# The first layer of the experts as three products of rounded parts, in one transformer block on one core

## What is computed

```python
# 16 experts, cap = 256 rows each, d = 256, H = 1024, all float32
buf = jnp.zeros((n_exp, cap, d), x.dtype).at[idx, safe_pos].add(jnp.where(keep[:, None], xf, 0.0))
h = jax.nn.relu(jnp.einsum('ecd,edh->ech', buf, W1) + b1[:, None, :])
y = jnp.einsum('ech,ehd->ecd', h, W2) + b2[:, None, :]
out = y[idx, safe_pos] * gate[:, None]
```

## Time and profile before

| | |
|---|---|
| median of 3 runs | 1383.31 us (1381.31 to 1388.11) |
| the profiled execution | 1389.05 us, of which the span from first to last instruction 1387.2 us |
| TensorE busy | 1235.2 us (89%) |
| VectorE, ScalarE, GpSimd busy | 824.6, 573.5, 326.3 us |
| mean granted TensorE clock | 0.942 |
| the chain that ended last, by engine | PE 67%, issue 11%, ACT 6%, DMA 5%, DVE 5% |

### The profile page before, as it was taken

The page is one execution under the profiler, slowest core; times in us unless marked ns, Lnnn a source line. Parts: engine busy times, 40 slices in busy tenths (PEclk is TensorE's granted clock), DMA queues, the critical chain, the costliest instruction groups (busy, mean ns, idle before and its releaser), DMA issues.

```text
span 1387.2 us, 24033 instructions
## 1 busy us (share of the span) xinstructions
PE 1235.2 (89%) x7258; PEld 864.4 (62%) x7258; DVE 824.6 (59%) x2163; ACT 573.5 (41%) x1387; POOL 326.3 (24%) x488
## 2 busy tenths in 40 slices
PE   4588888888999999999999999999988529999995
PEld 1455555655666666666666666666656428888884
DVE  6356666666667766666667666666655623444443
ACT  2245555545555555555555555555540001111110
POOL 3111121111233332222333212222212520111111
PEclk7689999999999999999999999999999759999998
DMA  5311112111221222122122211212257852565630
GB/s 188 129 66 58 66 57 80 50 38 44 78 71 64 69 78 73 54 68 79 57 72 66 82 54 61 76 53 68 76 183 261 271 182 87 196 235 174 232 103 18
DMA packets 100150, 139.29 MB, mean 100 GB/s; under 512 B 9980, under 2 KB 71294, under 8 KB 99968
## 3 DMA queue, kind: packets, MB, share of 16 engines
q1 hardware_dynamic: 91536, 113.55, 24.9%
q10 hardware_dynamic: 4464, 16.25, 2.9%
q0 software_dynamic: 4096, 8.82, 1.6%
HBM read 94.50 MB, written 48.00 MB: 103 GB/s over the span
## 4 chain that ended last, share of the span: by engine, by line
PE 67%; issue 11%; ACT 6%; DMA 5%; DVE 5%; POOL 3%; SPq 2%; DVEq 0%; ACTq 0%; POOLq 0%
PE SC L676 16%; PE Z L694 14%; PE Z L841 8%; PE SC L815 8%; ACT E L876 5%; PE XA L648 5%; PE XA L726 4%; PE XA L658 3%; PE XB L658 3%; DMA xln<-in_x 3%; PE XB L648 2%; POOL Wvl L1371 1%; PE XB L713 1%; DMA out<-th 1%; POOL slots_s L1476 1%
## 5 line engine op out<-in xcount | busy, mean ns | idle before, releaser
L876 ACT ACTIVATE E<-SC,nm 128x512 f32<-128x512 f32 (+7 forms) x512 | 375.1, 739 | 426.3 <-DVE nm L1089 426.3
L1089 DVE CUSTOM_DVE_ANT_0 SC<-SC,mask 128x512 f32<-128x512 f32 (+7 forms) x512 | 375.9, 786 | 205.4 <-PE SC L676 204.2
L676 PE MATMUL SC<-XQ,XK 64*128 64x512 f32 (+3 forms) x2304 | 270.0, 366 | 55.7 <-ACT E L876 54.1
L676 PEld LDWEIGHTS SC<-XQ,XK 64*128 64x128 f32 x2304 | 187.7, 190 | 155.5 <-issue 138.6
L694 PE MATMUL Z<-E,vs 128*64 128x512 f32 (+3 forms) x1536 | 271.9, 496 | 3.0 <-DVE vs L1067 3.0
L694 PEld LDWEIGHTS Z<-E,vs 128*64 128x64 f32 x1536 | 100.3, 138 | 140.9 <-issue 128.1
L841 PE MATMUL Z<-W,hh 128*128 128x256 f32 x512 | 114.9, 383 | 2.2 <-DVE yb L1335 2.2
L815 PE MATMUL SC<-bT,W 128*128 128x256 f32 x512 | 114.7, 383 | 0.0
L815 PEld LDWEIGHTS SC<-bT,W 128*128 128x128 f32 x512 | 98.5, 193 | 13.7
L841 PEld LDWEIGHTS Z<-W,hh 128*128 128x128 f32 x512 | 97.3, 192 | 15.6 <-DVE yb L1335 2.6
L876 ACT ACTIVATION_READ_ACCUMULATOR E<-SC,nm 128x1 f32 x512 | 101.1, 197 | 0.0
(11 more groups left out here) (191 smaller groups left out, 1720.7 us busy)
## 6 DMA issues: line engine op xcount, KB each, us to landing
W<-in_w SPq DMA_DIRECT2D x32, 1024.0 KB, 8.4
z_s<-zs ACTq DMA_DIRECT2D x31, 512.0 KB, 2.6
zt<-z_s SPq DMA_DIRECT2D x24, 512.0 KB, 3.8
W<-in_wqk SPq DMA_DIRECT2D x33, 257.0 KB, 2.7
slots_s<-zt SPq DMA_DIRECT2D x16, 520.0 KB, 3.9
xb<-slots_s SPq DMA_DIRECT2D x16, 520.0 KB, 3.7
xb<-xh_s SPq DMA_DIRECT2D x24, 256.0 KB, 4.7
Wv<-in_wv SPq DMA_DIRECT2D x17, 256.0 KB, 2.7
```

Source lines behind the costliest of these rows:

```text
L676: last = pe.matmul(SC[h][:, at:at + z - a], XK[rows, ap, kp, lo:lo + P], XQ[rows, ap, qp, a:z], start=(t == 0), stop=(t == 2))
L876: act.activation(E[:, h, EOFF[kb]:EOFF[kb + 1]], SC[h][:, at:at + S - lo], ACT.Exp, bias=nm[:, h, kb:kb + 1], scale=-1.0, accum_out=rs[:, ...
L1089: dve.tensor_tensor_reduce(SC[h][:, at:at + S - lo], SC[h][:, at:at + S - lo], mask[:, 0:S - lo], 1.0, BIG, ALU.add, ALU.min, nm[:, h, kb: ...
```

## The change

The first layer of each expert is computed in the way of the projections: from `W1h`, the rounded weights, `W1l`, the weights less those, `bTh`, the rounded rows, and `bTl`, the rows less those, as three products of type `float32r`.

- **TensorE**: `hidden` has 48 products in place of 16, and waits for `w1_hi`, `w1_lo`, `bT_done` and `bT_low`. The wait for `we_in` (now 48: without `W1`) stands ahead of the second layer. `transpose_rows` waits for `bT_low` in place of `bT_done`.
- **ScalarE**: `rows` writes `bTh`; behind it `weights_high` writes `W1h`, 128x2048 values, from `W1`. Its `hidden` waits for `we_in`.
- **VectorE**: `rows_low` and `weights_low` write `bTl` and `W1l` behind `hidden` and ahead of `grow`.
- **SyncE**: `W1` has two buffers in place of four, its own semaphores `w1_in`, and a load of its own, `load_first_weights`. For experts 0 and 1 it is issued where it was, for 2 and 3 behind the four `load_slots` in place of the middle of the second stage, and from 4 on at the place where it was; from 2 on it waits until the split of the expert two before is done.
- **SBUF**: `W1l` lies over `th`, so VectorE waits for `tail_scattered` and `tail_out` before the first split.

```diff
-        W1 = sb("W1", [P, NW, NC, HID])
+        W1 = sb("W1", [P, 2, NC, HID])
+        W1h = sb("W1h", [P, 2, NC, HID], F32R)
...
-        bT = sb("bT", [P, 2, NC, CAP])
+        bTh = sb("bTh", [P, 2, NC, CAP], F32R)
+        bTl = sb("bTl", [P, 2, NC, CAP], F32R)
...
-        th = sb("th", [P, TAIL, ROW])
+        rows_left = ExitStack()
+        th = sb("th", [P, TAIL, ROW], stack=rows_left)
+        rows_left.close()
+        past, top[0] = top[0], place["th"]
+        W1l = sb("W1l", [P, 2, NC, HID], F32R)
+        sb("left_of_th", [P, (past - top[0]) // 4])
...
+        w1_in = [sem(f"w1_in{k}") for k in range(2)]
+        w1_hi = sem("w1_hi")
+        w1_lo = sem("w1_lo")
+        bT_low = sem("bT_low")
...
+        def load_first_weights(eng, e, k):
+            eng.dma_start(W1[:, k % 2, :, :], w1_d[e].rearrange("(c p) n -> p c n", p=P)).then_inc(w1_in[k % 2], 16)
         def load_expert(eng, e, k):
...
-            eng.dma_start(W1[:, k, :, :], w1_d[e].rearrange("(c p) n -> p c n", p=P)).then_inc(we_in[k], 16)
...
             for k in range(2):
+                load_first_weights(sp, k, k)
...
             for k in range(NW):
...
+            for k in range(2, NW):
+                sp.wait_ge(w1_hi, k - 1)
+                sp.wait_ge(w1_lo, k - 1)
+                load_first_weights(sp, k, k)
...
                 for k in range(NW):
...
+                    sp.wait_ge(w1_hi, e - 1)
+                    settle(sp, sp_passed)
+                    sp.wait_ge(w1_lo, e - 1)
+                    settle(sp, sp_passed)
+                    load_first_weights(sp, e, k)
...
         @block.tensor
...
             def hidden(e, j, k):
-                pe.wait_ge(we_in[k], 64 * (j + 1))
+                pe.wait_ge(w1_hi, e + 1)
+                pe.wait_ge(w1_lo, e + 1)
...
+                pe.wait_ge(bT_low, e + 1)
...
+                        col = (2 * m + half) * P
...
-                            col = (2 * m + half) * P
-                            last = pe.matmul(hid[m][:, half * CAP:(half + 1) * CAP], W1[:, k, c, col:col + P],
-                                             bT[:, k % 2, c, :], start=(c == 0), stop=(c == NC - 1))
+                            for n, (w, x) in enumerate(((W1h, bTh), (W1h, bTl), (W1l, bTh))):
+                                last = pe.matmul(hid[m][:, half * CAP:(half + 1) * CAP], w[:, k % 2, c, col:col + P],
+                                                 x[:, k % 2, c, :], start=(c == 0 and n == 0), stop=(c == NC - 1 and n == 2))
...
             def transpose_rows(e, j, k):
...
-                    pe.wait_ge(bT_done, e - 1)
+                    pe.wait_ge(bT_low, e - 1)
...
+                pe.wait_ge(we_in[k], 48 * (j + 1))
...
             def rows(e, k):
...
-                act.activation(bT[:, k % 2, :, :], xbT[k % 2][:, :].rearrange("p (c t) -> p c t", c=NC), ACT.Copy).then_inc(bT_done, 1)
-            def hidden(e, k):
+                act.activation(bTh[:, k % 2, :, :], xbT[k % 2][:, :].rearrange("p (c t) -> p c t", c=NC), ACT.Copy).then_inc(bT_done, 1)
+            def weights_high(e, j, k):
+                act.wait_ge(w1_in[k % 2], 16 * (NW // 2 * j + k // 2 + 1))
+                if not isinstance(e, int) or e > 1:
+                    act.wait_ge(hid_mm[3], e - 1)
+                act.activation(W1h[:, k % 2, :, :], W1[:, k % 2, :, :], ACT.Copy).then_inc(w1_hi, 1)
+            def hidden(e, j, k):
+                act.wait_ge(we_in[k], 48 * (j + 1))
...
             def expert(j, k):
...
-                    hidden(e + 1, (k + 1) % NW)
+                    hidden(e + 1, j + (k + 1) // NW, (k + 1) % NW)
...
+                    weights_high(e + 2, j + (k + 2) // NW, (k + 2) % NW)
+            weights_high(0, 0, 0)
+            weights_high(1, 0, 1)
...
-            hidden(0, 0)
+            hidden(0, 0, 0)
...
         @block.vector
...
-            def hidden(e, k):
+            xbT = [XA, XB]
+            def weights_low(e, k):
+                dve.wait_ge(w1_hi, e + 1)
+                dve.tensor_tensor(W1l[:, k % 2, :, :], W1[:, k % 2, :, :], W1h[:, k % 2, :, :].bitcast(F32), ALU.subtract).then_inc(w1_lo, 1)
+            def rows_low(e, k):
+                dve.wait_ge(bT_done, e + 1)
+                dve.tensor_tensor(bTl[:, k % 2, :, :], xbT[k % 2][:, :].rearrange("p (c t) -> p c t", c=NC),
+                                  bTh[:, k % 2, :, :].bitcast(F32), ALU.subtract).then_inc(bT_low, 1)
+            def hidden(e, j, k):
+                dve.wait_ge(we_in[k], 48 * (j + 1))
...
             def expert(j, k):
...
-                    hidden(e + 1, (k + 1) % NW)
+                    hidden(e + 1, j + (k + 1) // NW, (k + 1) % NW)
+                if not isinstance(e, int) or e + 2 < NE:
+                    rows_low(e + 2, (k + 2) % NW)
+                    weights_low(e + 2, (k + 2) % NW)
...
-            hidden(0, 0)
+            dve.wait_ge(tail_scattered, 16 * TPB)
+            dve.wait_ge(tail_out, 48)
+            weights_low(0, 0)
+            rows_low(0, 0)
+            rows_low(1, 1)
+            weights_low(1, 1)
+            hidden(0, 0, 0)
...
         @block.gpsimd
```

## The result

| | before | after |
|---|---|---|
| median (runs) | 1385.71 us (1381.31 to 1388.49, 4 runs) | 1362.08 us (1360.75 to 1365.12, 4 runs) |
| ratio of after to before | | 0.9837, 95% interval 0.9811 to 0.9863 |
| span of the profiled execution | 1387.2 us | 1363.4 us |

Forecast were 1364.5 us and 18.8 us less than before. The medians above differ by 23.6 us, and the interval, on 1385.71, is 19 to 26 us less. Later measurements with more runs of both kernels gave 20.1 us (1383.29 to 1363.19) and 20.0 (1384.34 to 1364.33), so by these the forecast is short by one to two.

A forecast was written before the change was run, and what follows sets the result against it. TensorE was taken to bound the experts' stage: 1.20 us less for each of 16 experts, 19.2, minus 0.4 at the start, gives 18.8 us off the median of 1383.31, so 1364.5 us. The range was 1356 to 1378.

The forecast's parts named there:

- The bound: Experts' stage: TensorE's three blocks alone make the chain, 14.26 us per expert, so its savings are gained in full.
- The pace: First layer on TensorE: 48 rounded products at line 658's 0.1173 us each, 5.63 us in place of 6.91.
- first rival: First layer: products at 0.108 us, no cost for the change of kind, 27.6 - 0.4 us saved, 1356.1; chance 0.05.
- The rule: TensorE: N/2.4 + 2.5 ns per matmul, 0.1092 us for 256 columns; saving 1.67 us per expert, 26.7 in all.
- The change of kind: TensorE, first product behind float32 work: 0.083 us more per expert, bounds 0 and 0.083.
- The splits: ScalarE's weights_high 1.88 us, VectorE's weights_low 2.29, with handoffs 4.29 inside 6.11 us before the next first layer; slack 1.8.
- second rival: TensorE's wait for w1_lo: splits taking twice as long end last, 14 us slower, 1397; chance 0.05.
- The loads: SyncE's W1 loads: issued 4.3 us after the second layer, 15.5 us allowed, 5.8 to 11.9 taken, 3.6 slack.
- third rival: Two W1 buffers starve the experts' stage: 12 loads at 17 us cost 18 and leave 1383; chance 0.07.
- The start: Before the first first-layer block: rows_low delays it from 1141.49 to 1141.87 us, cost 0.4 us.
- The first block: Experts 0 and 1: 15.49 us for what takes 13.82 at full clock; the loss of 1.67 left as is.
- The end: Last second layer unchanged: waits 2.2 us for yb, then takes 8.88 us instead of 6.92.

The follow-up runs named there:

- e5: Changed kernel with the W1 splits of experts 2 to 15 cut from 1024 to 8 columns of each half; ratio 0.984 to the kernel before.
- e7: Changed kernel without the third product (weights' rest by rounded rows), 32 products per expert in place of 48; 1333.47 us, ratio 0.9621.
- e6: Changed kernel with weights_high and weights_low each done twice per expert; 1417.5 us, ratio 1.0213 to the kernel before.
- e8: Changed kernel with the load of W1 behind its expert's other loads, from expert 4 on; ratio 0.9843 to the kernel before.
- e1: The changed kernel again, no edit, for its spread and a second trace; median 1363.19 us, ratio 0.985.
- e11: The changed kernel again, no edit, as the measure for e9 and e10's call; median 1364.33 us, ratio 0.9858.
- e10: Changed kernel, second layer waiting for the output rows of expert e - 2 instead of e - 1; median 1360.34 us, ratio 0.9828.
- e9: Changed kernel with that relaxed wait and nine unused TensorE products ahead of the first transposes; median 1359.05 us, ratio 0.9813.

## Why the prediction was right

- **The bound** was named rightly: the chain had TensorE alone, and e5 (less work elsewhere: no gain) and e7 (fewer products: gain in full) show it from both sides.
- **The pace** of a rounded product, taken from line 658, was 0.1173 us and is 0.1170. The first rival, with 0.108, falls with it.
- **The rule.** The Trainium skill (TensorE: Matmul & The Clock Gate, section Back-to-back issue gap) gives the formula behind the estimate of 0.1092 us for a matmul by itself, and says that in a stream with weight loads both set the spacing. The prediction took the formula for such a stream; the trace has 0.1170 there and doesn't agree with it.
- **The change of kind**, 0.083 us per expert, is the term that was mis-sized. The first step of a block is longer in the records (0.31 us), but the block is 5.62 to 5.66 us, which is 48 x 0.117 with next to nothing added. So the saving is 1.27 us per expert in the 14 steps of experts 2 to 15 (206.45 us before, 188.73 after), 17.7 us where the forecast had 16.8. I had put the lower bound, 0, beside it.
- **The splits** took 1.90 and 2.29 us for the 1.88 and 2.29 extrapolated from 512 and 1024 columns. The slack was 1.8 us as forecast, counted to the next layer's first record as the prediction did. The second rival's place and its mechanism are those of e6; its price was too low, since it left out the clock: 53 to 55 us over the changed kernel, where the rival had 32.
- **The loads** are asked for 4.2 us behind the second layer (1185.68 to 1189.88; forecast 4.3) and land in 11.0 at most, with 15.5 allowed. e8 bears the third rival out as no danger.
- **The start**: from the first transposes to the first block the records show 2.12 us before and 2.60 after, 0.5 us more (forecast 0.4). By the chain it is 0.3.
- **The first block** of experts 0 and 1: I left its loss to the clock at 1.67 us. In this trace it was 2.5 (13.72 us for 96 x 0.117), so the block gave 1.8 us and not 2.4. In e1 and e11 it took 12.41 and 12.60.
- **The end**: I left the last block at 8.88 us. It was 7.16 in this trace, at a granted clock of 1.00 from 1344 to 1351 us, and 8.83 in e1's, where the clock is 0.50 from 1336.7 to 1339. So up to 1.7 us of one trace's gain is a matter of when the clock falls.
- **The sum**, from the first transposes to the end, by the chain. Forecast: 16.8 for the 14 steps, 2.4 for the first block, 0.4 lost at the start, nothing at the end, 18.8. This trace: 17.7, 1.8, 0.3 lost, 1.6, together 20.8. e1's trace: 17.7, 3.1, 0.3 lost, 0.1 lost, together 20.4. The 17.7 is the mechanism as forecast, and it is the same in both; the first block and the end move by 1 to 2 us with the clock, and that they add up to about the same in both, 3.4 and 3.0 where the forecast had 2.4, is luck.

## What to carry to other kernels

When one engine makes up the whole chain of a stage and its records are even, a change can be priced in records of the same types and shape from another stage, and the price of one record held to a fraction of a per cent here (0.1173 for 0.1170 us). The price of the change between kinds, taken from one step of the records, did not hold: the step was there, and the block was no longer for it. What has to be worked out as carefully is the cover: the time from the moment that the added work's input exists to the moment that the bound engine asks for its result. And when two traces differ in a stage that the change hardly touches, more traces of each, and the medians of many runs, tell more than a story.

## What the runs showed of the hardware

- Rounded products run at 0.117 us per 256 columns at a granted clock of 1.00 (46 steps in 5.38 us), and the 512-column ones of line 648 at 0.233 (10 steps from 600.50 to 602.83 us of the first trace before): 0.456 to 0.457 ns per column in both. The float32 records, two per instruction, stand 0.216 us apart for the same 256 columns. Three rounded products cost 0.351 us where one float32 instruction costs 0.432.
- In e6 each of 14 first layers came behind a gap of 2.2 to 2.3 us in TensorE's work. In 13 of them the granted clock fell to 0.50 (1.2 GHz; 0.21 us per product) 0.4 to 1.5 us after the work had begun again, for 14 to 16 steps of the products; in one it stayed 1.00. The gap ahead of the last layer is of the same length. Behind it the last block took 0.25 us more than 6.91 in the first trace of the changed kernel, with the clock at 1.00, and 1.9 to 2.0 us more in e1, e11 and the three traces before.
